# Wo's sixteen low parts: from POOL's queue to DVE's, behind the seventh head's high part

## The chip, the core and the metric

The kernel runs on one core of a Trainium2 chip. The metric is the device time of one execution in microseconds (us), as the median of several runs. The engines are called PE (TensorE matmul), PEld (its weight load), DVE (VectorE), ACT (ScalarE), POOL (GpSimd) and SP (SyncE, which issues the DMAs).

## What is computed

A decoder layer on 16 sequences of 112 tokens, width 1024, with a layer norm behind each of its three parts: a gated feed-forward part that keeps only the larger half of its gate, cross attention to 375 context rows with 32 query heads and 8 key/value heads, and a dequantized 4-bit linear layer. The change lies in the attention:

```
def _L0_xattn_ref(query, key, value, Wq, Wk, Wv, Wo):
    ...
    scores = jnp.einsum('bhqd,bhkd->bhqk', q, k) * scale
    probs = jax.nn.softmax(scores, axis=-1)
    out = jnp.einsum('bhqk,bhkd->bhqd', probs, v)
    out = out.transpose(0, 2, 1, 3).reshape(b, sq, DIM)
    return out @ Wo
```

Products in fp32 are made of three passes in a faster format: an operand is split into a high part, which is its value rounded to that format, and a low part, the fp32 value minus the high part. So each operand needs two element-wise instructions before PE can use it, a cast and a subtraction.

## The kernel before

Four passes run one after the other: the context pass (keys and values), the gated and query pass, `attend_pass` (1839 to 2223 us of the profile) and `finish_pass`. The change is in `attend_pass`.

`attend_pass` goes over 16 batches n (a batch is one sequence) and in each over 8 key/value heads h, each with its 4 query heads. g = 8n + h counts the heads through, x = 3h + t the steps of a batch (24 of them, KT = 3 to a head). At a step PE makes one block of scores (`ap_p_t`, L1663), one third of the product with the values of the head three behind (`ap_p_o`, L1682, or L1676 for a head that isn't split), and at 16 of the 24 steps a pair of matmuls `ap_p_s` (L1648) from which the softmax maximum of the next batch is taken. What each engine does for them:

- ACT: the exponential `ap_e` of each block (L1529), the high part `ap_e_hi` of heads 1, 2 and 4 (L1536), the copy of finished output, and Wo's high parts `wo_wo_hi` (L1547).
- DVE: the maxima of the pairs (L1577, 16 to a batch, called y0 to y15), the high part of heads 0, 5, 6 and 7 (L1591), in batches 4, 8 and 12 a reciprocal (L1597), and the low parts from head 119 on (L1609).
- POOL: the low part `ap_e_lo` of every split head up to 118 (L1509), seven to a batch, since head 3 isn't split.
- Wo comes as 16 half blocks of 128x512 (`ap_wo_raw`, two buffers): two in batch 0 and one in each of batches 1 to 14. ACT makes the high part behind the last exponential of head 6, and POOL the low part (`wo_wo_lo`, L1496), ahead of head 6's own low part. Both are first read in `finish_pass`.

Each engine works through its own queue in the order of the code; nothing reorders it, and semaphores alone hold an instruction back. Pair y of the next batch may be written when the maximum of pair y-2 is taken, because `ap_p_s` has two buffers. Pairs y0 and y1 stand at steps 22 and 23 of a batch, y2 to y15 at steps 1, 2, 4 to 7 and 9 to 16 of the next. `ap_e_hi` and `ap_e_lo` have three buffers, `ap_e` four. PE reads the low part of head g in the middle step of the head g+3.

In the functions printed below, `split_w` of the POOL program makes Wo's low parts, `maxima` and `split_hi` of the DVE program are the instructions that the new one joins, and `first_pair`, `scores` and `values` are PE's.

Of the kernel before, what the change touches and what calls it, by code (L numbers as in the profile page):

```python
# [6 lines left out]
F32 = mybir.dt.float32  # L7
# [4 lines left out]
ALU = mybir.AluOpType  # L12
# [15 lines left out]
H, KV, HD = 32, 8, 32  # L28
REP = H // KV
KT = 3  # L30
# [137 lines left out]
def tile_loads(i):  # L168

    return 2 * (((i + 1) * P - 1) // S - i * P // S + 1) + REP  # L170
# [1154 lines left out]
def attend_pass(nc, cy, kd, vd, qd, w_o, wo_hi, wo_lo, ident_f, od, rd):  # L1325
# [18 lines left out]
    W_LOAD_AT, W_SPLIT_AT = 3, 6  # L1344
# [10 lines left out]
    def hi_by_dve(g):  # L1355
        return split(g) and not hi_by_act(g)

    def lo_by_dve(g):
        return split(g) and g >= KV * (B - 1) - 1

    def lo_by_pool(g):
        return split(g) and not lo_by_dve(g)

    def upto(kind, g):

        return sum(kind(x) for x in range(g + 1))

    def cols(k):
        return slice(D // 2 * (k % 2), D // 2 * (k % 2 + 1))

    def w_parts(n):

        return (0, 1) if n == 0 else (n + 1,) if n < B - 1 else ()

    with ExitStack() as ctx:
# [7 lines left out]
        wo_raw = [m.sb(f"wo_raw{i}", [P, D // 2], F32) for i in range(2)]  # L1383
# [18 lines left out]
        def pairs_at(n, x):  # L1402

            if x in PAIR_OF:
                found = n + 1, PAIR_OF[x]
            elif x - NX in PAIR_OF:
                found = n + 2, PAIR_OF[x - NX]
            else:
                return ()
            return (found,) if found[0] < B else ()  # L1410

        def await_hi(eng, g):
            if not split(g):
                eng.wait_ge(exped, KT * (g + 1))
            elif hi_by_act(g):
                eng.wait_ge(hi_act, upto(hi_by_act, g))
            else:
                eng.wait_ge(hi_dve, upto(hi_by_dve, g))
# [70 lines left out]
        @block.gpsimd  # L1489
        def _(pool):  # L1490
            nc.gpsimd.memset(ks[1][STACK:KR].bitcast(F32), 1.0).then_inc(ones, 1)
            pool.wait_ge(ones, 2)

            def split_w(k):
                pool.wait_ge(wo_hi_done, k + 1)
                nc.gpsimd.tensor_tensor(wo_lo[:, k // 2, cols(k)], wo_raw[k % 2][:], wo_hi[:, k // 2, cols(k)].bitcast(F32),  # L1496
                                        ALU.subtract).then_inc(wo_lo_done, 1)
                pool.wait_ge(wo_lo_done, k + 1)

            for g in range(KV * B):  # L1500
                if g % KV == W_SPLIT_AT:
                    pool.wait_ge(lo_pool, upto(lo_by_pool, g - 1))
                    for k in w_parts(g // KV):
                        split_w(k)
                if lo_by_pool(g):
                    await_hi(pool, g)
                    if g >= NLO:
                        pool.wait_ge(pv, g - NLO + 1)
                    nc.gpsimd.tensor_tensor(e_lo[g % NLO][:], e[g % NE][:], e_hi[g % NHI][:].bitcast(F32),  # L1509
                                            ALU.subtract).then_inc(lo_pool, 1)  # L1510
            pool.wait_ge(cy.hi_done, 1)
            nc.gpsimd.tensor_tensor(cy.o_lo[:], cy.num[:], cy.o_hi[:].bitcast(F32), ALU.subtract).then_inc(cy.lo_done, 1)
# [57 lines left out]
        @block.vector  # L1570
        def _(dve):
            def maxima(n, y):
                h, a = divmod(y, 2)
                if y == 0 and n > 0:
                    dve.wait_ge(nm_turned, n)
                dve.wait_ge(scored, NPAIR * n + y + 1)
                nc.vector.reduce_max(n_max[:, h // 2, 2 * a:2 * a + 2, h % 2], p_s[y % 2][:, :, 0:C], AX_X).then_inc(maxed, 1)  # L1577

            def max_lo(n):
                dve.wait_ge(nmh, n + 1)  # L1580
                nc.vector.scalar_tensor_tensor(out=nm_lo[:], in0=p_s[0][0:H, 0, 384:384 + S], scalar=-1.0,
                                               in1=nm_hi[:].bitcast(F32), op0=ALU.mult,
                                               op1=ALU.subtract).then_inc(nml, 1)

            def split_hi(g):
                dve.wait_ge(exped, KT * (g + 1))
                if g >= NHI:
                    dve.wait_ge(pv, g - NHI + 1)
                if upto(hi_by_dve, g) > 1:
                    dve.wait_ge(hi_dve, upto(hi_by_dve, g) - 1)  # L1590
                nc.vector.tensor_scalar(e_hi[g % NHI][:], e[g % NE][:], 1.0, None, ALU.mult, ALU.add,  # L1591
                                        accum_out=e_sum[:]).then_inc(hi_dve, 1)

            def invert(c):
                for i in range(NO):
                    dve.wait_ge(o_put[i], PUT * cy.pairs_out(i, GB * (c + 1)))
                nc.vector.reciprocal(den[c % 2][:], den[c % 2][:]).then_inc(recip, 1)  # L1597

            def quotients():

                dve.wait_ge(cy.o_loaded[0], 16 * tile_loads(0))
                nc.vector.tensor_tensor(cy.num[:], cy.num[:], cy.add[:], ALU.add)
                dve.drain()
                nc.vector.tensor_tensor(cy.num[:], cy.num[:], cy.rec[:], ALU.mult).then_inc(cy.normed, 1)

            def split_lo(g):
                await_hi(dve, g)
                dve.wait_ge(pv, g - NLO + 1)
                nc.vector.tensor_tensor(e_lo[g % NLO][:], e[g % NE][:], e_hi[g % NHI][:].bitcast(F32),  # L1609
                                        ALU.subtract).then_inc(lo_dve, 1)  # L1610

            def follow(g):
                if hi_by_dve(g):
                    split_hi(g)
                if lo_by_dve(g):
                    split_lo(g)

            for x in range(NX + PAIR_AT[0], NX):
                for pair in pairs_at(-1, x):
                    maxima(*pair)  # L1620
            for n in range(B):
                for x in range(NX):
                    h, t = divmod(x, KT)
                    for pair in pairs_at(n, x):
                        maxima(*pair)
                    if t == 0 and KV * n + h >= 1:
                        follow(KV * n + h - 1)
                    if x == RECIP_AT and n % GB == 0 and n > 0:
                        invert(n // GB - 1)
                    if x == TURN_AT + 2 and n + 1 < B:  # L1630
                        max_lo(n + 1)
                    if n == B - 1 and x == QUOTIENTS_AT:
                        quotients()
            follow(KV * B - 1)

        @block.tensor
# [380 lines left out]
```

## Time and profile before

| what | us |
|---|---|
| median of 3 runs | 2459.7 (2456.05 to 2464.17) |
| the profiled execution, its own time | 2460.78 |
| span of that execution | 2459.0 |
| POOL busy in the span | 1382.4 |
| DVE busy in the span | 1270.6 |

All times of instructions are us from the start of the span. A start and a length of an instruction are as the profiler recorded them; the next instruction of an engine may begin some hundredths before the recorded end of the one ahead. "[0.78 <-ACT ap_e_hi L1536]" behind a row means that the engine was idle for 0.78 us in front of it and that ACT's instruction released it.

### The profile page before, as it was taken

How to read it: one execution, taken by the hardware profiler on the slowest of the kernel's cores; microseconds unless marked ns; L12 is line 12 of the kernel's file. 1: busy time of each engine (PE TensorE's matmuls, PEld its weight loads, DVE VectorE, ACT ScalarE, POOL GpSimd, SP SyncE). 2: the span in 40 equal slices, each digit the busy share in tenths (PEclk: the TensorE clock that was granted, in tenths of full speed). 3: DMA queues.
4: the chain of work that ended last, by engine and by line, in shares of the span. 5: the costliest groups of instructions: out<-in, count | busy, mean ns of one | idle time of the engine just before them, and what ended most of it. 6: DMA issues, size and time to landing. Idle time of an engine off the chain costs nothing. (4 is left out here: it accounts for less than half of the span.)

```text
span 2459.0 us, 33124 instructions
## 1 busy us (share of the span) xinstructions
PE 2403.3 (98%) x12798; PEld 2093.2 (85%) x12798; DVE 1270.6 (52%) x1785; ACT 1045.2 (43%) x1539; POOL 1382.4 (56%) x627
## 2 busy tenths in 40 slices
PE   9999999999999999999999999999999999998998
PEld 9999999988899888999889998899986666666775
DVE  5862304862016940048610269335538888884665
ACT  2112235533337342355333373323327888882111
POOL 5434244866446855448654468445438999971221
PEclk9999999999999999999999999999999999999999
DMA  7656632234323333323343223369986667667672
GB/s 228 193 167 189 197 108 95 104 124 131 111 102 103 127 100 125 109 102 103 116 131 118 94 103 112 107 212 279 297 218 178 189 195 201 181 172 189 174 175 88
DMA packets 256014, 371.74 MB, mean 151 GB/s; under 512 B 127184, under 2 KB 179408, under 8 KB 255600
## 3 DMA queue, kind: packets, MB, share of 16 engines
q1 hardware_dynamic: 255856, 369.61, 49.6%
q8 instruction: 102, 1.67, 0.3%
q14 instruction: 56, 0.46, 0.1%
HBM read 290.15 MB, written 78.70 MB: 150 GB/s over the span
## 5 line engine op out<-in xcount | busy, mean ns | idle before, releaser
L1028 POOL TENSOR_TENSOR gp_w_lo<-cy_raw,gp_w_hi 128x1024 fp32r<-128x1024 f32 (+2 forms) x299 | 721.0, 2412 | 608.5 <-ACT gp_w_hi L903 608.0
L187 PE MATMUL gp_acc<-gp_x_hi,gp_w_hi 128*128 128x448 f32 x1504 | 558.7, 371 | 2.6 <-ACT gp_row L954 2.5
L188 PE MATMUL gp_acc<-gp_x_lo,gp_w_hi 128*128 128x448 f32 x1504 | 550.3, 366 | 0.0
L189 PE MATMUL gp_acc<-gp_x_hi,gp_w_lo 128*128 128x448 f32 x1504 | 550.1, 366 | 0.0
L903 ACT CAST gp_w_hi<-cy_raw 128x1024 fp32r<-128x1024 f32 (+2 forms) x300 | 307.2, 1026 | 314.2 <-PE gp_acc L189 308.4
L1509 POOL TENSOR_TENSOR ap_e_lo<-ap_e,ap_e_hi 125x1344 fp32r<-125x1344 f32 x104 | 317.2, 3082 | 21.3 <-ACT ap_e_hi L1536 14.2
L187 PEld LDWEIGHTS gp_acc<-gp_x_hi,gp_w_hi 128*128 128x128 f32 x1504 | 283.2, 188 | 26.0 <-ACT gp_row L954 4.0
L189 PEld LDWEIGHTS gp_acc<-gp_x_hi,gp_w_lo 128*128 128x128 f32 x1504 | 282.9, 188 | 22.2
L188 PEld LDWEIGHTS gp_acc<-gp_x_lo,gp_w_hi 128*128 128x128 f32 x1504 | 283.3, 188 | 20.9
L514 DVE TENSOR_REDUCE gp_sel_unit<-gp_keys 112x4 f32<-112x2048 f32 x4 | 9.1, 2286 | 547.8 <-ACT gp_keys L915 547.8
L187 PE MATMUL gp_acc<-gp_h_hi,gp_w_hi 128*128 128x448 f32 (+1 forms) x704 | 266.8, 379 | 8.4 <-DVE gp_h_lo L1091 5.6
L189 PE MATMUL gp_acc<-gp_h_hi,gp_w_lo 128*128 128x448 f32 (+1 forms) x704 | 258.3, 367 | 0.0
L188 PE MATMUL gp_acc<-gp_h_lo,gp_w_hi 128*128 128x448 f32 (+1 forms) x704 | 258.0, 366 | 0.0
L1577 DVE TENSOR_REDUCE cy_n_max<-ap_p_s 112x2 f32<-112x750 f32 x240 | 220.2, 936 | 28.8 <-PE ap_p_s L1648 26.3
L1529 ACT ACTIVATE ap_e<-ap_p_t 125x448 f32<-125x448 f32 x384 | 205.5, 546 | 68.7 <-PE ap_p_t L1663 63.6
L507 DVE TENSOR_SCALAR_CACHE_REDUCE gp_keep<-gp_keys,gp_sel_bound 112x2752 bf16<-112x2752 f32 (+1 forms) x56 | 158.2, 2867 | 64.3 <-ACT gp_keys L915 61.7
L341 POOL TENSOR_TENSOR cp_c_lo<-cp_c_raw,cp_c_hi 128x1504 fp32r<-128x1504 f32 x30 | 103.9, 3484 | 140.1 <-ACT cp_c_hi L311 140.1
L921 ACT ACTIVATE gp_act<-gp_acc 128x448 f32<-128x448 f32 x84 | 45.7, 544 | 272.3 <-PE gp_acc L189 272.3
L1663 PE MATMUL ap_p_t<-cy_qs,cy_ks 98*125 98x448 f32 x384 | 156.6, 409 | 0.4 <-DMA cy_qs<-cy_nm_lo 0.3
L187 PEld LDWEIGHTS gp_acc<-gp_h_hi,gp_w_hi 128*128 128x128 f32 (+1 forms) x704 | 132.7, 188 | 23.5 <-DVE gp_h_lo L1091 6.8
L189 PEld LDWEIGHTS gp_acc<-gp_h_hi,gp_w_lo 128*128 128x128 f32 (+1 forms) x704 | 132.5, 188 | 11.7
L188 PEld LDWEIGHTS gp_acc<-gp_h_lo,gp_w_hi 128*128 128x128 f32 (+1 forms) x704 | 132.9, 189 | 10.0
(212 smaller groups left out, 4307.0 us busy)
## 6 DMA issues: line engine op xcount, KB each, us to landing
cy_raw<-in_w_gu SPq DMA_DIRECT2D x172, 512.0 KB, 3.2
cy_raw<-in_w_d SPq DMA_DIRECT2D x80, 512.0 KB, 3.5
cp_c_raw<-in_ctx_t SPq DMA_DIRECT2D x30, 750.0 KB, 7.0
cy_raw<-in_w_q SPq DMA_DIRECT2D x32, 512.0 KB, 4.2
q_scratch<-gp_q_out SPq DMA_DIRECT2D x64, 224.0 KB, 6.3
cy_qs<-q_scratch SPq DMA_DIRECT2D x64, 224.0 KB, 3.4
k_scratch<-cp_k_out SPq DMA_DIRECT2D x32, 376.0 KB
cy_ks<-k_scratch SPq DMA_DIRECT2D x64, 188.0 KB, 3.5
```

The source lines that it names most:

```text
L187: nc.tensor.matmul(out, wh, xh, start=first, stop=False)
L188: nc.tensor.matmul(out, wh, xl, start=False, stop=False)
L189: return nc.tensor.matmul(out, wl, xh, start=False, stop=last)
L341: nc.gpsimd.tensor_tensor(c_lo[p][:, ks(h), :], c_raw[p][:, ks(h), :], c_hi[p][:, ks(h), :].bitcast(F32), ALU.subtract).then_inc(lo_done, 1)
L507: self.nc.vector.tensor_scalar(self.keep[:, b, 0:width], self.keys[:, b, 0:width], bound[:, b:b + 1], None, op, ALU.add, accum_out=self.co ...
L903: last = nc.scalar.copy(o, i)
L921: nc.scalar.activation(act_t[:, c, :], a[:, 0:T], ACT.Silu).then_inc(evac, 1)
L1028: last = nc.gpsimd.tensor_tensor(o, i, hi.bitcast(F32), ALU.subtract)
L1509: nc.gpsimd.tensor_tensor(e_lo[g % NLO][:], e[g % NE][:], e_hi[g % NHI][:].bitcast(F32), ALU.subtract).then_inc(lo_pool, 1)
L1529: nc.scalar.activation(e[g % NE][:, x % KT, :], p_t[x % 2][0:KN, 0:T], ACT.Exp, scale=SCALE).then_inc(exped, 1)
L1577: nc.vector.reduce_max(n_max[:, h // 2, 2 * a:2 * a + 2, h % 2], p_s[y % 2][:, :, 0:C], AX_X).then_inc(maxed, 1)
L1663: nc.tensor.matmul(p_t[x % 2][0:KN, 0:T], ks[p][0:KR, h // 2, h % 2, t * KN:(t + 1) * KN], qs[p][:, h // 2, :, h % 2, :], start=True, stop ...
```

## The change

The subtraction for Wo's half blocks is issued on DVE in place of POOL, with the same operands. It stands at step 21, where the seventh head's (h = 6) high part has just been issued, and waits for ACT's high part of the block. POOL's queue keeps only the low parts of the heads, and loses two waits for itself around each block.

```
@@ POOL's program
-            def split_w(k):
-                pool.wait_ge(wo_hi_done, k + 1)
-                nc.gpsimd.tensor_tensor(wo_lo[:, k // 2, cols(k)], wo_raw[k % 2][:], wo_hi[:, k // 2, cols(k)].bitcast(F32),
-                                        ALU.subtract).then_inc(wo_lo_done, 1)
-                pool.wait_ge(wo_lo_done, k + 1)
-
             for g in range(KV * B):
-                if g % KV == W_SPLIT_AT:
-                    pool.wait_ge(lo_pool, upto(lo_by_pool, g - 1))
-                    for k in w_parts(g // KV):
-                        split_w(k)
@@ DVE's program
+            def split_w(k):
+                dve.wait_ge(wo_hi_done, k + 1)
+                nc.vector.tensor_tensor(wo_lo[:, k // 2, cols(k)], wo_raw[k % 2][:], wo_hi[:, k // 2, cols(k)].bitcast(F32),
+                                        ALU.subtract).then_inc(wo_lo_done, 1)
+
...
+                    if x == KT * (W_SPLIT_AT + 1):
+                        for k in w_parts(n):
+                            split_w(k)
```

POOL's queue in batch 0 before, from head 5's low part on, with what each instruction waits for:

```order
L1509 TENSOR_TENSOR ap_e_lo_18197<-ap_e_18203,ap_e_hi_18194 125x1344 [waits ap_pv,ap_hi_dve]
L1496 TENSOR_TENSOR wo_wo_lo<-ap_wo_raw_18200,wo_wo_hi 128x512 [waits ap_wo_hi_done,ap_lo_pool]
L1496 TENSOR_TENSOR wo_wo_lo<-ap_wo_raw_18201,wo_wo_hi 128x512 [waits ap_wo_hi_done,ap_wo_lo_done]
L1509 TENSOR_TENSOR ap_e_lo_18195<-ap_e_18204,ap_e_hi_18192 125x1344 [waits ap_pv,ap_hi_dve,ap_wo_lo_done]
L1509 TENSOR_TENSOR ap_e_lo_18196<-ap_e_18205,ap_e_hi_18193 125x1344 [waits ap_pv,ap_hi_dve]
```

The same place after; the low parts of heads 5, 6 and 7 now follow one another:

```order
L1499 TENSOR_TENSOR ap_e_lo_18197<-ap_e_18203,ap_e_hi_18194 125x1344 [waits ap_pv,ap_hi_dve]
L1499 TENSOR_TENSOR ap_e_lo_18195<-ap_e_18204,ap_e_hi_18192 125x1344 [waits ap_pv,ap_hi_dve]
L1499 TENSOR_TENSOR ap_e_lo_18196<-ap_e_18205,ap_e_hi_18193 125x1344 [waits ap_pv,ap_hi_dve]
```

DVE's queue in batch 0 before, from the low part of the negated maxima (`cy_nm_lo`) on; 112x2 rows are the maxima, 125x1344 the high parts of heads 6, 7 and 0 of the next batch:

```order
L1581 SCALAR_TENSOR_TENSOR cy_nm_lo<-ap_p_s,cy_nm_hi 32x112 [waits cy_nmh]
L1591 TENSOR_SCALAR ap_e_hi_18192,ap_e_sum<-ap_e_18204 125x1344 [waits ap_hi_dve,ap_pv,ap_exped]
L1577 TENSOR_REDUCE cy_n_max<-ap_p_s 112x2 [waits cy_scored,cy_nm_turned]
L1577 TENSOR_REDUCE cy_n_max<-ap_p_s 112x2 [waits cy_scored]
L1591 TENSOR_SCALAR ap_e_hi_18193,ap_e_sum<-ap_e_18205 125x1344 [waits ap_hi_dve,ap_pv,ap_exped]
L1577 TENSOR_REDUCE cy_n_max<-ap_p_s 112x2 [waits cy_scored] x2
L1591 TENSOR_SCALAR ap_e_hi_18194,ap_e_sum<-ap_e_18202 125x1344 [waits ap_hi_dve,ap_pv,ap_exped]
```

And after; the lines are numbered anew:

```order
L1571 SCALAR_TENSOR_TENSOR cy_nm_lo<-ap_p_s,cy_nm_hi 32x112 [waits cy_nmh]
L1581 TENSOR_SCALAR ap_e_hi_18192,ap_e_sum<-ap_e_18204 125x1344 [waits ap_hi_dve,ap_pv,ap_exped]
L1604 TENSOR_TENSOR wo_wo_lo<-ap_wo_raw_18200,wo_wo_hi 128x512 [waits ap_wo_hi_done]
L1604 TENSOR_TENSOR wo_wo_lo<-ap_wo_raw_18201,wo_wo_hi 128x512 [waits ap_wo_hi_done]
L1567 TENSOR_REDUCE cy_n_max<-ap_p_s 112x2 [waits cy_scored,cy_nm_turned]
L1567 TENSOR_REDUCE cy_n_max<-ap_p_s 112x2 [waits cy_scored]
L1581 TENSOR_SCALAR ap_e_hi_18193,ap_e_sum<-ap_e_18205 125x1344 [waits ap_hi_dve,ap_pv,ap_exped]
```

The two subtractions stand between head 6's high part and the maximum y0, so y0, y1 and head 7's high part are queued behind them. In batches 1 to 14 it is one.

## Rows read from the trace of the kernel before

**Rows 1.** The page: busy time, share of the span, instructions.
```profile
PE 2403.3 (98%) x12798; PEld 2093.2 (85%) x12798; DVE 1270.6 (52%) x1785; ACT 1045.2 (43%) x1539; POOL 1382.4 (56%) x627
```

**Rows 2.** Line L1509: durations in ns (min/median/max); who waited, us and times.
```profile
L1509 POOL TENSOR_TENSOR ap_e_lo<-ap_e,ap_e_hi x104: 3048/3082/3117, 1847.7 to 2199.2; 125x1344 fp32r<-125x1344 f32 x104
...
  PEld ap_p_o L1682: 38.2, 64
  PE ap_p_o L1682: 13.4, 15
```

**Rows 3.** Timeline of POOL (start us, us, engine, line, operation).
```profile
1865.75 2.67 POOL L1496 TENSOR_TENSOR wo_wo_lo<-ap_wo_raw,wo_wo_hi 128x512 fp32r<-128x512 f32 x2
...
1890.71 1.28 POOL L1496 TENSOR_TENSOR wo_wo_lo<-ap_wo_raw,wo_wo_hi 128x512 fp32r<-128x512 f32 x1
...
2008.67 1.29 POOL L1496 TENSOR_TENSOR wo_wo_lo<-ap_wo_raw,wo_wo_hi 128x512 fp32r<-128x512 f32 x1
...
2026.09 6.12 POOL L1509 TENSOR_TENSOR ap_e_lo<-ap_e,ap_e_hi 125x1344 fp32r<-125x1344 f32 x2 [0.78 <-ACT ap_e_hi L1536]
...
2150.34 1.29 POOL L1496 TENSOR_TENSOR wo_wo_lo<-ap_wo_raw,wo_wo_hi 128x512 fp32r<-128x512 f32 x1
...
2168.05 6.09 POOL L1509 TENSOR_TENSOR ap_e_lo<-ap_e,ap_e_hi 125x1344 fp32r<-125x1344 f32 x2 [1.09 <-ACT ap_e_hi L1536]
2174.22 1.28 POOL L1496 TENSOR_TENSOR wo_wo_lo<-ap_wo_raw,wo_wo_hi 128x512 fp32r<-128x512 f32 x1
...
2197.81 1.29 POOL L1496 TENSOR_TENSOR wo_wo_lo<-ap_wo_raw,wo_wo_hi 128x512 fp32r<-128x512 f32 x1
2199.18 3.06 POOL L1509 TENSOR_TENSOR ap_e_lo<-ap_e,ap_e_hi 125x1344 fp32r<-125x1344 f32 x1
```

**Rows 4.** Timeline of DVE in batch 6, from head 6's high part on.
```profile
2006.43 1.55 DVE L1591 TENSOR_SCALAR_CACHE_REDUCE ap_e_hi<-ap_e 125x1344 fp32r<-125x1344 f32 x1 [0.39 <-PE ap_p_o L1676]
...
2007.98 1.83 DVE L1577 TENSOR_REDUCE cy_n_max<-ap_p_s 112x2 f32<-112x750 f32 x2
2009.73 1.54 DVE L1591 TENSOR_SCALAR_CACHE_REDUCE ap_e_hi<-ap_e 125x1344 fp32r<-125x1344 f32 x1
...
2014.37 3.60 DVE L1577 TENSOR_REDUCE cy_n_max<-ap_p_s 112x2 f32<-112x750 f32 x4
```

**Rows 5.** Timeline of ACT in the same batch: Wo's high part.
```profile
2006.07 0.60 ACT L1547 CAST wo_wo_hi<-ap_wo_raw 128x512 fp32r<-128x512 f32 x1
```

**Rows 6.** Timeline of PEld: the weight load of pair y6 in that batch.
```profile
2015.35 0.27 PEld L1648 LDWEIGHTS ap_p_s<-cy_ks,cy_qs 96*112 96x112 f32 x2 [0.28 <-DVE cy_n_max L1577]
```

**Rows 7.** Timelines of DVE (y0) and PEld (y6) in batch 4, with a reciprocal.
```profile
1960.77 0.94 DVE L1577 TENSOR_REDUCE cy_n_max<-ap_p_s 112x2 f32<-112x750 f32 x1
```
```profile
1968.79 0.27 PEld L1648 LDWEIGHTS ap_p_s<-cy_ks,cy_qs 96*112 96x112 f32 x2 [0.94 <-DVE cy_n_max L1577]
```

**Rows 8.** Timelines of DVE (y0) and PE (y6) in batch 12, with a reciprocal.
```profile
2150.01 0.94 DVE L1577 TENSOR_REDUCE cy_n_max<-ap_p_s 112x2 f32<-112x750 f32 x1 [0.35 <-issue]
```
```profile
2158.03 0.61 PE L1648 MATMUL ap_p_s<-cy_ks,cy_qs 96*112 96x376 f32 x2 [0.85 <-DVE cy_n_max L1577]
```

**Rows 9.** Timelines of POOL and DVE in the gated pass.
```profile
515.10 1.17 POOL L1039 TENSOR_TENSOR gp_act<-gp_act,gp_row 128x448 f32<-128x448 f32 x1
518.05 2.40 POOL L1028 TENSOR_TENSOR gp_w_lo<-cy_raw,gp_w_hi 128x1024 fp32r<-128x1024 f32 x1 [1.78 <-ACT gp_w_hi L903]
520.41 1.53 POOL L1039 TENSOR_TENSOR gp_act<-gp_act,gp_row 128x448 f32<-128x448 f32 x1
```
```profile
518.10 2.84 DVE L1091 TENSOR_TENSOR gp_h_lo<-gp_h,gp_h_hi 128x448 fp32r<-128x448 f32 x1
```

**Rows 10.** Line L1091: durations in ns (min/median/max).
```profile
L1091 DVE TENSOR_TENSOR gp_h_lo<-gp_h,gp_h_hi x88: 606/642/2845, 516.8 to 1583.5; 128x448 fp32r<-128x448 f32 x84, 64x448 fp32r<-64x448 f32 x4
```

**Rows 11.** Timeline of DVE: its own low parts of heads 119 and 120.
```profile
2199.35 4.31 DVE L1609 TENSOR_TENSOR ap_e_lo<-ap_e,ap_e_hi 125x1344 fp32r<-125x1344 f32 x1
...
2205.16 1.56 DVE L1609 TENSOR_TENSOR ap_e_lo<-ap_e,ap_e_hi 125x1344 fp32r<-125x1344 f32 x1
```

## The prediction

> **What bounds the kernel now.** I read the page's busy times first, then the line of the low parts, then the timelines of the engines in one batch of the attention pass. The page doesn't decide anything here: POOL has 56% and DVE 52% of the span [rows 1], but these are averages over four passes. In the attention pass POOL sets the pace. Its low parts take 3.08 us each, and PE waited 38.2 us at its weight loads and 13.4 us at its matmuls for them [rows 2]. Its work comes round once a batch: Wo's low part starts at 1890.71 in batch 1 and at 2197.81 in batch 14, thirteen rounds of 23.62 us on the mean [rows 3]. A round of POOL is seven low parts, Wo's subtraction of 1.29 with its 0.08 wait for itself (2008.67 to the next low part), and 0.78 in which it waits for head 4's high part from ACT [rows 3].
>
> The reader should see a second loop beside it, nearly as long, that doesn't go through POOL's arithmetic but through DVE and PE. From y0 on DVE works without a break: y0 and y1 from 2007.98, head 7's high part at 2009.73, four more maxima from 2014.37 [rows 4], and PE waits for one of these (y4) before it may load pair y6, at 2015.35 [rows 6]. From y6 PE goes on to the scores of head 4, ACT makes its exponential and high part, and POOL's low part of head 4 waits for that. Of this loop I take the parts from rows:
>
> - y0's start to y6's start: 2007.98 to 2015.35, 7.37 us [rows 4, 6]. With a reciprocal in between (batches 4, 8 and 12) it is 8.02: 1960.77 to 1968.79 and, again, 2150.01 to 2158.03 [rows 7, 8].
> - y6 to the start of head 4's low part: 2158.03 to 2168.05, 10.02 us [rows 3, 8]. I take it from batch 12 because PE met no wait for POOL in it, so it is PE's own pace.
> - the low parts of heads 4 and 5: 6.10 us (6.09 recorded for the two; Wo's part starts 6.17 behind their start, less some 0.07 of waiting for itself) [rows 3].
>
> Call L the moment at which POOL is free after head 5's low part, 0.07 ahead of the row of Wo's low part. In batch 6 L is 2008.60, and y0 starts at L - 0.62. The second loop is then -0.62 + 7.37 + 10.02 + 6.10 = 22.87, that is 0.75 shorter than POOL's 23.62. It is hidden. Batch 12 shows it bare: there y0 starts at L - 0.26, the sum is -0.26 + 8.02 + 10.02 + 6.10 = 23.88, and the round measured 2150.34 to 2174.22, 23.88 [rows 3, 8].
>
> **What the change removes.** 16 instructions on POOL of 1.29 us with 0.08 of waiting, 1.37 each and 21.9 us in all [rows 3]. If nothing else moved, all of it would come off POOL's path.
>
> **What it adds on DVE.** No row shows this shape on DVE. The nearest is the same subtraction with 448 columns, at 0.606 when undisturbed [rows 10]. With 1344 columns it takes 1.56 [rows 11]. By the slope between the two, 0.95 us for 896 columns, 512 columns take about 0.67 recorded, and the next instruction can start some 0.08 sooner: 0.60. That is not what it will cost, however. At 518.10 this subtraction was started on DVE while POOL was in one of its own, and took 2.84; it ended at 520.94, 0.53 behind the start of POOL's next instruction, which had been queued and whose start was recorded at 520.41 [rows 9]. In the attention pass the same: 4.31 instead of 1.56, when POOL was busy from 2199.18 for 3.06 [rows 3, 11]. So DVE waits until POOL's instruction is over and then gets through first, and the queued POOL instruction pays: 1.53 against 1.17 for the same shape, 0.36 to 0.38 for 448 columns, some 0.45 for 512. The Trainium skill says this in "SBUF — State Buffer", section "Who interferes with whom": a DVE instruction with two SBUF inputs contends with a GpSimd instruction that reads SBUF, and one of them fully blocks. By that rule the trace agrees (2.84 us against 0.61). The maxima and the high parts of rows 4 keep their durations beside POOL.
>
> **Where it lands.** Head 6's high part ends on DVE at 2007.98, Wo's high part has been there since 2006.67 [rows 4, 5], so the subtraction is ready at L - 0.62, in the middle of POOL's low part of head 5, and must wait for L. It ends near L + 0.58, and y0 starts 0.08 sooner, at L + 0.50 (448 columns: 520.94 - 0.08 - 520.41 = 0.45, and 0.05 to 0.07 for 64 more). This holds in every batch: head 6's high part follows PE, and POOL's low parts of heads 4 and 5 start when PE and ACT let them, so their distance stays. Queued behind the subtraction are y0, y1, head 7's high part, y2 and y3, head 0's high part and y4. PE waits for y4. y0 moves from L - 0.62 to L + 0.50, 1.12 later, and only 0.75 of that was slack.
>
> The new round is 0.50 + 7.37 + 10.02 + 6.10 = 23.99, against 23.62: +0.37. POOL's own round would be 23.62 - 1.37 + 0.45 = 22.70, so POOL is no longer what ends last. With a reciprocal: 0.50 + 8.02 + 10.02 + 6.10 = 24.64, against 23.62 twice and 23.88 once: +1.02, +1.02 and +0.76.
>
> **Batch 0** has two subtractions in a row. Before, its round took 1865.75 to 1890.71, 24.96 [rows 3]. After the first one POOL's low part of head 6 is queued and waiting. If it goes first, DVE's second waits for it: y0 at L + 0.45 + 3.05 + 0.50 = L + 4.00, a round of 27.49, +2.53. If DVE runs both at a stretch, y0 is at L + 1.10, a round of 24.59, -0.37. No row shows that case. In rows 9 it was the engine that had waited that came next, so I take +2.53.
>
> **The end.** Behind batch 14's subtraction (L near 2197.74) there are no pairs left. DVE's low part of head 119 waits for POOL's low part of head 118, which starts 1.37 sooner and is held up 0.45: -0.9.
>
> **Sum:** 2.53 + 10 x 0.37 + 1.02 + 1.02 + 0.76 - 0.9 = +8.1 us. The finishing pass keeps its order. The profiled execution took 2460.78 around a span of 2459.0, and would take 2468.9; its time is 1.1 above the median of the three runs, so the median becomes 2459.7 + 8.1 = 2467.8 us. About 0.3%, 7.4 us, is what a measurement of this kernel can tell from no change, so this is on the edge.
>
> **Rivals.**
>
> 1. Batch 0's two subtractions run at a stretch: 2.9 less, +5.2, 2464.9 us. Against it only rows 9, for it that DVE's next instruction is recorded as starting 0.08 before the end of the one ahead.
> 2. POOL stays the bound and the change is a gain. This needs a looser second loop than I read: DVE's delay would have to be taken up before y6, though rows 4 show no gap there. The round is then 22.70, -0.92 in thirteen rounds and some -1.8 in batch 0, with -0.9 at the end: -14.7, 2445.0 us. It decides from a second loop of 22.7 or less, so my loop would be 1.3 too long. Batch 12, where the sum met the measured round, speaks against it. The Trainium skill's "GPSIMD Engine Reference", section "Engine selection", advises it: element-wise work on a tile belongs on VectorE, GpSimd being about twice as slow with two inputs. Rows 10 and 3 agree on the speed (0.67 against 1.29); what they don't give is the port and the place.
> 3. DVE is not blocked at this place. y0 starts at L - 0.02, the round is 23.47, 24.12 with a reciprocal: 10 x -0.15, +0.5, +0.5, +0.24, -0.9 in batch 0, -1.4 at the end, -2.6 us, 2457.1. Against it stand rows 9 and 11.
> 4. DVE loses the turn to POOL's queued low part of head 6 in each batch: y0 at L + 3.55, 3.05 more in thirteen rounds, +48 us, near 2508. Rows 9 show the other order.
>
> **How the numbers follow.** The forecast has 0.45, rival 1 0.27, rival 2 0.12, rival 3 0.10, rival 4 0.06. The round's terms carry 0.1 us or so together, 1.3 us over thirteen rounds, and the first term alone may be 0.45 or 0.60, so the forecast's own range is 2465 to 2471. About a third of it lies below the 0.3% line, and nearly all of rivals 1 and 3: same 0.44. Slower is the rest of the forecast, and rival 4, with a little of rival 1: 0.43. Faster is rival 2 and a little of rival 3: 0.13. The range from 2456 to 2472 holds the forecast, rivals 1 and 3, and leaves out rivals 2 and 4 with 0.18.
>
> **What would show it.** On DVE the sixteen subtractions take between 1.1 and 1.5 us recorded (0.62 of waiting and 0.67), not 0.67, and in batch 0 the second takes some 3.6. POOL's low part of head 6 is recorded at 3.5 instead of 3.08. POOL's idle time in a round grows from 0.8 to 2.1 or so, 1.6 of it in front of head 4's low part. PE no longer waits for POOL's low parts, or for a few us in all in place of 51, and waits for DVE's maxima at y2, y4 and y6 instead. The round of POOL is 24.0, 24.6 at batches 4, 8 and 12. Wrong would be: a round under 23.6; PE still waiting for POOL; subtractions of 0.67 on DVE; or subtractions of more than 3 us in every batch.

## The result, and the profile after

The changed kernel took 2467.8 us in the median of six runs (2463.85 to 2469.41), the kernel before 2459.1 in the seven beside them. The ratio is 1.0035, 95% interval 1.0025 to 1.0045: slower by some 8.6 us, where +8.1 was forecast. One more execution of the changed kernel, slow by far at 12134.81 us, is left out; with it the median is 2468.9, the number that an expectation below quotes. The profiled execution took 2466.65 around a span of 2464.9. The attention pass is 7.9 us longer in it: from POOL's first low part to the finishing pass it was 1847.74 to 2225.92 before, 378.2, and is 1845.08 to 2231.18, 386.1. The finishing pass took 233.7 against 233.1, and the passes ahead of attention happened to end 2.7 earlier.

The page of the changed kernel, busy time, share and instructions of each engine, to be held against [rows 1]:

```profile
PE 2401.3 (97%) x12798; PEld 2095.8 (85%) x12798; DVE 1287.2 (52%) x1801; ACT 1046.1 (42%) x1539; POOL 1369.6 (56%) x611
```

Sixteen instructions moved from POOL to DVE. POOL lost 12.8 us and not the 20.6 of sixteen times 1.29, and DVE gained 16.6 and not the 10.7 of sixteen times 0.67. The other two views show where the rest sits: first the line of POOL's low parts (durations in ns, minimum, median, maximum; what ended POOL's idle time; who waited), then the line of DVE's subtractions.

```profile
L1499 POOL TENSOR_TENSOR ap_e_lo<-ap_e,ap_e_hi x104: 3050/3086/3552, 1845.1 to 2203.9; 125x1344 fp32r<-125x1344 f32 x104
...
  ACT ap_e_hi L1526: 26.8, 16
  DVE ap_e_hi L1581: 15.6, 15
...
  PEld ap_p_o L1680: 0.8, 1
  PE ap_p_o L1680: 0.4, 1
```
```profile
L1604 DVE TENSOR_TENSOR wo_wo_lo<-ap_wo_raw,wo_wo_hi x16: 1222/1229/3520, 1862.1 to 2203.3; 128x512 fp32r<-128x512 f32 x16
```

PE's waits for POOL's low parts have gone: 0.8 us and 0.4 in place of the 38.2 and 13.4 of [rows 2]. The waits of the attention pass (1842 to 2210; us in all, times, longest) name who took POOL's place:

```profile
PEld ap_p_s L1646 <- DVE cy_n_max L1567: 30.9, 32, 3.8
POOL ap_e_lo L1499 <- ACT ap_e_hi L1526: 26.8, 16, 2.6
PE ap_p_s L1646 <- DVE cy_n_max L1567: 24.5, 31, 3.4
```

Batch 6 shows one round. DVE's timeline from the subtraction on, PEld's at pair y6, and POOL's over the round (start us, us; in brackets the idle time ahead and what ended it), beside [rows 3, 4, 6]:

```profile
2010.77 1.22 DVE L1604 TENSOR_TENSOR wo_wo_lo<-ap_wo_raw,wo_wo_hi 128x512 fp32r<-128x512 f32 x1
2011.92 1.77 DVE L1567 TENSOR_REDUCE cy_n_max<-ap_p_s 112x2 f32<-112x750 f32 x2
...
2034.63 1.24 DVE L1604 TENSOR_TENSOR wo_wo_lo<-ap_wo_raw,wo_wo_hi 128x512 fp32r<-128x512 f32 x1
```
```profile
2019.22 0.27 PEld L1646 LDWEIGHTS ap_p_s<-cy_ks,cy_qs 96*112 96x112 f32 x2 [1.37 <-DVE cy_n_max L1567]
```
```profile
2005.36 9.58 POOL L1499 TENSOR_TENSOR ap_e_lo<-ap_e,ap_e_hi 125x1344 fp32r<-125x1344 f32 x3 [1.68 <-ACT ap_e_hi L1526]
2015.24 12.37 POOL L1499 TENSOR_TENSOR ap_e_lo<-ap_e,ap_e_hi 125x1344 fp32r<-125x1344 f32 x4 [0.29 <-DVE ap_e_hi L1581]
2029.22 9.60 POOL L1499 TENSOR_TENSOR ap_e_lo<-ap_e,ap_e_hi 125x1344 fp32r<-125x1344 f32 x3 [1.61 <-ACT ap_e_hi L1526]
```

The subtraction starts at 2010.77, in the middle of POOL's low part of head 5, and ends at 2011.99, some 0.5 behind that part's end (2005.36 and twice 3.05 give 2011.46). It had been started by then, so it was no semaphore that held it back. POOL's three low parts then last 9.58 instead of 9.16 or so: 3.48 for the third. POOL waits 1.61 ahead of head 4 in place of 0.78. The round is 2010.77 to 2034.63, 23.86.

Batch 0 has two subtractions. DVE's, PE's and POOL's timelines there, then two windows (length, busy time and instructions of PE, PEld, DVE, ACT and POOL, the granted clock, DMA share, GB/s):

```profile
1862.08 4.67 DVE L1604 TENSOR_TENSOR wo_wo_lo<-ap_wo_raw,wo_wo_hi 128x512 fp32r<-128x512 f32 x2
```
```profile
1867.66 0.97 PE L1646 MATMUL ap_p_s<-cy_ks,cy_qs 96*112 96x376 f32 x2 [3.35 <-DVE cy_n_max L1567]
1868.42 0.57 PE L1661 MATMUL ap_p_t<-cy_qs,cy_ks 98*125 98x448 f32 x1
...
1874.27 0.36 PE L1661 MATMUL ap_p_t<-cy_qs,cy_ks 98*125 98x448 f32 x1
```
```profile
1869.99 6.24 POOL L1499 TENSOR_TENSOR ap_e_lo<-ap_e,ap_e_hi 125x1344 fp32r<-125x1344 f32 x2 [3.79 <-DVE ap_e_hi L1581]
```
```profile
1863.00:1868.00 5.00, 1.65 (x8) 1.00 (x7) 5.00 (x4) 1.57 (x4) 3.21 (x1) 0.88 0.93 273
1868.00:1875.00 7.00, 7.00 (x24) 5.49 (x24) 6.55 (x9) 2.92 (x6) 4.89 (x2) 0.60 0.57 145
```

The two subtractions took 4.67 together, PE stood for 3.35 behind them, and the clock fell from 2.4 to 1.2 GHz, at the end of that wait already (0.88 over 1863 to 1868): matmuls of 448 columns last 0.57 instead of 0.36, until some 1873.7. Before, PE stood 2.08 at most behind 1863 and kept a clock of 1.00.

A mark that every kernel below has is DVE's row on cy_nm_lo, once a batch. The round of batch 0 from these is 1862.86 to 1887.82 before, 24.96, and here:

```profile
1859.95 0.26 DVE L1571 SCALAR_TENSOR_TENSOR cy_nm_lo<-ap_p_s,cy_nm_hi 32x112 fp32r<-32x112 f32 x1 [0.47 <-ACT cy_nm_hi L1509]
1888.48 0.26 DVE L1571 SCALAR_TENSOR_TENSOR cy_nm_lo<-ap_p_s,cy_nm_hi 32x112 fp32r<-32x112 f32 x1 [0.47 <-ACT cy_nm_hi L1509]
...
1960.16 0.26 DVE L1571 SCALAR_TENSOR_TENSOR cy_nm_lo<-ap_p_s,cy_nm_hi 32x112 fp32r<-32x112 f32 x1 [0.47 <-ACT cy_nm_hi L1509]
1984.76 0.26 DVE L1571 SCALAR_TENSOR_TENSOR cy_nm_lo<-ap_p_s,cy_nm_hi 32x112 fp32r<-32x112 f32 x1 [0.47 <-ACT cy_nm_hi L1509]
```

Batch 0's takes 28.53, batch 4's, with a reciprocal, 24.60.

### The profile page after: what moved, and what is told of

Same layout as the page of the kernel before. It is cut to its first block and busy times, and to the rows that moved or that the text cites. A ratio compares the mean times of both kernels' runs of the same rounds, so it can differ in the third digit from the quotient of the medians.

```text
span 2464.9 us, 33107 instructions
## 1 busy us (share of the span) xinstructions
PE 2401.3 (97%) x12798; PEld 2095.8 (85%) x12798; DVE 1287.2 (52%) x1801; ACT 1046.1 (42%) x1539; POOL 1369.6 (56%) x611
## 5 line engine op out<-in xcount | busy, mean ns | idle before, releaser
L1499 POOL TENSOR_TENSOR ap_e_lo<-ap_e,ap_e_hi 125x1344 fp32r<-125x1344 f32 x104 | 324.6, 3148 | 43.7 <-ACT ap_e_hi L1526 26.8
L187 PEld LDWEIGHTS gp_acc<-gp_h_hi,gp_w_hi 128*128 128x128 f32 (+1 forms) x704 | 132.7, 188 | 23.2 <-DVE gp_h_lo L1091 6.8
L1646 PE MATMUL ap_p_s<-cy_ks,cy_qs 96*112 96x376 f32 x480 | 127.2, 347 | 25.0 <-DVE cy_n_max L1567 24.8
```

The lines of the kernel that those rows point to most:

```text
L187: nc.tensor.matmul(out, wh, xh, start=first, stop=False)
L1646: last = nc.tensor.matmul(p_s[y % 2][:, i, 0:CP], qs[p][0:STACK, f, 2 * a + i, h % 2, :], ks[p][0:STACK, f, h % 2, :], start=True, stop=True)
```

## The experiments

Theory: a subtraction on DVE waits for the end of the low part that POOL is in, and gets through ahead of POOL's next (called **the port** here). It so delays the maxima for which PE waits, and a **second loop** through DVE, PE and ACT, 22.87 us long when nothing delays it, sets the round. The rivals: the delay is only DVE's added work; POOL's arithmetic is still the bound; batch 0 is slow for another reason.

| run | median, before, us | ratio (95%) | plain round | round with reciprocal |
|---|---|---|---|---|
| changed kernel | 2467.8, 2459.1 | 1.0035 (1.0025 to 1.0045) | 23.9 | 24.6 |
| e1_one_input | 2457.75, 2458.09 | 0.9998 (0.9989 to 1.0008) | 23.35 | 24.05 |
| e2_two_quarters | 2511.32, 2458.09 | one run | 26.9 (28.0 in two) | 27.5 |
| e3_batch0_pool | 2462.32, 2458.09 | 1.0019 (1.001 to 1.0029) | 23.9 | 24.6 |
| e9_batch0_shared | 2465.75, 2460.4 | 1.0023 (1.0013 to 1.0032) | 23.9 | 24.6 |
| e7_act_copy | 2451.26, 2458.09 | 0.9977 (0.9968 to 0.9987) | 22.95 | 23.5 |
| e4_pool_ahead_of_4 | 2452.09, 2458.58 | 0.9977 (0.9968 to 0.9986) | 22.9 | 23.5 |
| e5_dve_before_y14 | 2453.24, 2458.58 | 0.9977 (0.9964 to 0.9989) | 22.9 | 23.5 |
| e6_pool4_recip20 | 2449.99, 2458.58 | 0.9967 (0.9955 to 0.9979) | 22.9 | 23.0 |
| e8_dve14_recip20 | 2453.76, 2460.4 | 0.997 (0.9959 to 0.9982) | 22.9 | 23.0 |

The rounds are those of most batches. e4, e5, e6 and e8 each have one or two that are 0.2 to 0.4 longer, at different batches. Batch 12's took 23.9 in the kernel before, in e7 and in e4, where DVE stood 0.35 for "issue" in front of y0 [rows 8], and 23.5 in e5. Why is open.

### One SBUF input instead of two (e1_one_input)

```diff
-                nc.vector.tensor_tensor(wo_lo[:, k // 2, cols(k)], wo_raw[k % 2][:], wo_hi[:, k // 2, cols(k)].bitcast(F32),
-                                        ALU.subtract).then_inc(wo_lo_done, 1)
+                if k > 0:
+                    dve.wait_ge(wo_lo_done, k)
+                nc.vector.tensor_scalar(wo_lo[:, k // 2, cols(k)], wo_raw[k % 2][:], 1.0, None, ALU.mult, ALU.add,
+                                        accum_out=w_sum[:]).then_inc(wo_lo_done, 1)
```

> From the changed kernel: DVE's instruction for Wo's half block stands at the same place and writes the same block, but reads one tensor in SBUF (a multiply by 1 with a sum, the form of the high parts) in place of two, so the low part isn't computed. Theory P (the port): the instruction takes 0.67 us recorded in place of 1.23, since it needn't wait for POOL; y0 starts 0.55 sooner behind head 6's high part, the round is 13.94 + 1.48 + 0.60 + 7.30 = 23.3 us (23.86 in the changed kernel), and batch 0's two take 1.3 together in place of 4.67. In all 10 x 0.55 + 3 x 0.55 + 3.5 = 10 to 11 us less than the changed kernel, 2458 us, about the time of before. Rival W (it is DVE's added work and its place, the port has no part in it): the round stays at 23.8 and the time at 2466 to 2469.

DVE's line of the sixteen instructions:

```profile
L1607 DVE TENSOR_SCALAR_CACHE_REDUCE wo_wo_lo<-ap_wo_raw x16: 679/681/686, 1864.1 to 2193.9; 128x512 fp32r<-128x512 f32 x16
```

The place, the queue and the size are the same; the second input from SBUF is gone, and with it the instruction has another form. The form isn't what counts: e5 below has the two-input subtraction at 0.68 as well, where POOL idles. The instruction takes 0.68, not 1.22 and never 3.52, also in batch 0; POOL's low parts are 9.16 for three. The round is 23.35 and the time that of the kernel before, to 0.1%. So DVE's added work alone doesn't make the kernel slower than before. It does lengthen the second loop, from 22.93 (e7, below) to 23.35, which is still under the 23.6 of before; the wait for POOL adds the other 0.54 and brings the round to 23.89. That this form passes POOL and the one with two inputs does not is as the Trainium skill's "SBUF — State Buffer", section "Who interferes with whom", has it.

### Two instructions of half the width (e2_two_quarters)

```diff
+                for i in range(2 if k >= 2 else 1):
+                    q = D // 4 if k >= 2 else D // 2
+                    c = D // 2 * (k % 2) + q * i
+                    done = nc.vector.tensor_tensor(wo_lo[:, k // 2, c:c + q], wo_raw[k % 2][:, q * i:q * i + q],
+                                                   wo_hi[:, k // 2, c:c + q].bitcast(F32), ALU.subtract)
+                done.then_inc(wo_lo_done, 1)
```

> From the changed kernel: in batches 1 to 14 the subtraction is two instructions of 256 columns, one behind the other, in place of one of 512. The work is the same but for some 0.1 us. Theory P, with the turn going to the engine that has waited: the first ends near L + 0.3, POOL's low part of head 6 goes next, and the second waits 3.05 us for it; y0 starts some 3.0 later than in the changed kernel, each round is 26.8 to 26.9, and the whole 40 to 44 us longer, near 2510 us. Rival S (DVE keeps the port for instructions at a stretch; batch 0's long second subtraction had another cause): the round stays within 0.2 of 23.9 and the time near 2470.

DVE's subtractions in batch 6, PE's matmuls of the scores behind the wait in batches 5 to 7, and the windows of the rounds of batches 0, 5, 6 and 7, each from mark to mark:

```profile
2027.44 4.15 DVE L1607 TENSOR_TENSOR wo_wo_lo<-ap_wo_raw,wo_wo_hi 128x256 fp32r<-128x256 f32 x2
```
```profile
2005.68 0.59 PE L1650 MATMUL ap_p_s<-cy_ks,cy_qs 96*112 96x376 f32 x2 [2.91 <-DVE cy_n_max L1567]
2032.50 0.97 PE L1650 MATMUL ap_p_s<-cy_ks,cy_qs 96*112 96x376 f32 x2 [2.80 <-DVE cy_n_max L1567]
2060.50 0.60 PE L1650 MATMUL ap_p_s<-cy_ks,cy_qs 96*112 96x376 f32 x2 [2.91 <-DVE cy_n_max L1567]
```
```profile
1862.90:1890.30 27.40, 23.98 (x106) 17.04 (x105) 25.25 (x27) 19.73 (x39) 21.82 (x8) 0.94 0.63 166
1998.48:2025.31 26.83, 22.52 (x106) 16.08 (x105) 24.75 (x28) 19.74 (x38) 21.54 (x8) 1.00 0.63 170
2025.31:2053.29 27.98, 25.18 (x106) 18.03 (x105) 25.06 (x27) 19.48 (x38) 21.58 (x8) 0.88 0.62 163
2053.29:2080.23 26.94, 23.98 (x106) 16.97 (x105) 24.76 (x28) 19.43 (x38) 21.53 (x8) 0.94 0.62 170
```

The same number of elements in two pieces costs 2.96 us a round (26.82 against 23.86): behind the first piece POOL's queued low part goes first, and the second piece waits for all of it. So between two instructions of DVE the engine that waits gets the turn. This was the open point in batch 0, and it is answered against rival 1.

The windows show more. PE's waits in batches 1 to 12 all lie between 2.80 and 2.93, but the granted clock of the round is 1.00 in two of them, 0.94 in eight and 0.88 in two. A short fall costs at most 0.1 (26.94 against 26.83), the long one 1.1 (27.98). In the long one the first matmul behind the wait is slow already (0.97); in the short ones it is at full speed, and the slow matmuls begin 1 to 3 us later.

Batch 0 is the same code here as in the changed kernel, with the same 4.67 of DVE and the same wait of 3.35. It took 27.40 with a clock of 0.94, where the changed kernel's took 28.53 with 0.88. What differs in the rows is how long the clock was low, so 1.13 of the 28.53 belong to that execution's clock.

### Batch 0's two back on POOL (e3_batch0_pool), or one of them (e9_batch0_shared)

```diff
-                    if x == KT * (W_SPLIT_AT + 1):
+                    if n > 0 and x == KT * (W_SPLIT_AT + 1):
```

and POOL's two subtractions of batch 0 as they were. The second run:

```diff
+                if g == W_SPLIT_AT:
+                    pool.wait_ge(lo_pool, upto(lo_by_pool, g - 1))
+                    pool.wait_ge(wo_lo_done, 1)
+                    split_w(1)
...
-                        for k in w_parts(n):
+                        for k in (0,) if n == 0 else w_parts(n):
```

> From the changed kernel: batch 0's two subtractions are POOL's again, the other fourteen stay on DVE. Theory P: batch 0's round goes from 28.5 us back to 25.0, the others stay at 23.86 (24.6 with a reciprocal): 3.5 us less than the changed kernel, some 4 us above before, 2463 to 2464 us. PE has no wait of over 3 us, and the granted clock in the 28 us behind batch 0's step 21 is 1.0 in place of 0.88. Rival: the later rounds make up for what batch 0 loses (slack behind it), then the time stays within 1 us of the changed kernel's.

> The changed kernel, but in batch 0 alone POOL makes the second of the two low parts, behind DVE's first and ahead of head 6's low part. What is told apart: whether batch 0 costs what it does (its round 28.5 us in place of 25.0, the 3.5 us instead of the forecast 2.53) because a second subtraction on DVE waits for a whole low part of POOL and PE, waiting 3.35 us behind it, loses its clock. By that: DVE's one subtraction there takes 1.2 us, PE waits for a maximum for less than 1.5 us in batch 0, no granted clock under 1.00 behind it, the round of batch 0 is 24 to 25 us, and the time 3.5 to 4.5 us under the changed kernel's 2468.9 less what the days differ: 2463 to 2464.5 beside 2459 for the kernel before. By the rival, that the clock falls there whatever DVE does (it is a slow stretch at the start of the pass), the clock's dip stays, the round is 25 to 26, and the time 2465 to 2466.

In the second run, DVE in batch 0 and the marks of its round, then the window behind:

```profile
1863.06 0.26 DVE L1581 SCALAR_TENSOR_TENSOR cy_nm_lo<-ap_p_s,cy_nm_hi 32x112 fp32r<-32x112 f32 x1 [0.47 <-ACT cy_nm_hi L1519]
...
1865.19 1.24 DVE L1614 TENSOR_TENSOR wo_wo_lo<-ap_wo_raw,wo_wo_hi 128x512 fp32r<-128x512 f32 x1
...
1887.25 0.26 DVE L1581 SCALAR_TENSOR_TENSOR cy_nm_lo<-ap_p_s,cy_nm_hi 32x112 fp32r<-32x112 f32 x1 [0.47 <-ACT cy_nm_hi L1519]
```
```profile
1868.00:1875.00 7.00, 5.57 (x28) 4.06 (x27) 7.00 (x10) 4.60 (x9) 7.00 (x3) 1.00 1.02 272
```

With one subtraction on DVE, batch 0's round is 24.19, its clock stays at 1.00 and PE waits 1.16 at most; with none it is 24.97. The rival, a stretch that is slow by itself, has fallen. The other rounds are 23.9 in both, so what is left in e3's ratio, 4.7 us, is the change's steady part. The step from 1.0035 to 1.0019 is 3.9 us, and the traces say 3.56 (28.53 against 24.97). The second run's median, 2465.75, lies in the range that its rival named, and not in the one expected; the kernel before took 2460.4 beside it, and by the ratio it is 5.7 us slower than before, where 4 to 5.5 were expected. It is the trace that decides against the rival. That trace is 4.34 shorter in batch 0 than the changed kernel's, the ratio only 0.0012 lower, 3 us, and no lower than e3's; the intervals leave room for both.

### No port, no POOL: a copy on ACT (e7_act_copy)

```diff
                 nc.scalar.copy(wo_hi[:, k // 2, cols(k)], wo_raw[k % 2][:]).then_inc(wo_hi_done, 1)
+                nc.scalar.copy(wo_lo[:, k // 2, cols(k)], wo_raw[k % 2][:]).then_inc(wo_lo_done, 1)
```

and DVE's subtractions left out.

> Neither POOL nor DVE makes Wo's low parts: ACT makes a second copy of the raw block in their place, behind the high part (0.52 us on ACT each, the low part isn't computed). It shows what taking the work off POOL is worth with DVE left alone. Theory L (the loop over DVE's maxima and PE is next, 22.8 to 22.9 us, 23.5 with a reciprocal): the round is 22.8 to 23.2, PE still waits little for POOL, and the time is 2459.1 - (0.4 to 0.8) x 13 - 2 = 2447 to 2452 us. Rival F (POOL alone sets the pace and all of its 1.37 us comes back): the round is 22.25, the time 2459.1 - 21 = 2438 us.

POOL's timeline over two rounds:

```profile
1995.87 21.35 POOL L1499 TENSOR_TENSOR ap_e_lo<-ap_e,ap_e_hi 125x1344 fp32r<-125x1344 f32 x7 [1.65 <-ACT ap_e_hi L1526]
2018.79 21.32 POOL L1499 TENSOR_TENSOR ap_e_lo<-ap_e,ap_e_hi 125x1344 fp32r<-125x1344 f32 x7 [1.57 <-ACT ap_e_hi L1526]
2041.73 6.10 POOL L1499 TENSOR_TENSOR ap_e_lo<-ap_e,ap_e_hi 125x1344 fp32r<-125x1344 f32 x2 [1.63 <-ACT ap_e_hi L1526]
```

POOL has only its seven low parts, 21.35, and nothing of Wo stands on DVE either. Still the round is 22.92 to 22.94, and POOL idles for 1.6 of it ahead of head 4. This is the second loop bare: 22.87 was worked out from rows of the kernel before, 22.93 is what it takes. So the change could not have gained more than some 0.7 a round, wherever its subtractions went, as long as the reciprocal stays where it is.

### Other places for the same subtraction (e4, e5, e6, e8)

POOL's own, but ahead of head 4's low part, where POOL idles (e4_pool_ahead_of_4, from the kernel before):

```diff
-                if g % KV == W_SPLIT_AT:
+                n, h = divmod(g, KV)
+                parts = w_parts(0) if g == W_SPLIT_AT else (n,) if n >= 2 and h == 4 else ()
+                if parts:
```

DVE's, but between the maxima of y13 and y14 of the next batch, when POOL idles (e5_dve_before_y14; batch 0's two on POOL):

```diff
+                    if x == 15 and n >= 2:
+                        split_w(n)
```

And each of the two with the reciprocal moved from between y0 and y6 to behind the low half of the maxima (e6_pool4_recip20, e8_dve14_recip20):

```diff
-                    if x == RECIP_AT and n % GB == 0 and n > 0:
+                    if x == TURN_AT + 2 and n % GB == 0 and n > 0:
```

> From the kernel before: the subtractions stay on POOL, but those of batches 1 to 14 are made in the next batch, ahead of head 4's low part, where POOL stands idle for 0.8 us a round waiting for ACT. Batch 0's two stay where they were. Theory L (POOL's queue and the loop over DVE's maxima and PE, 22.8 us): POOL's own round is 7 x 3.05 + 1.37 = 22.7, the other loop's 13.94 + 1.48 + 7.30 = 22.7 to 22.8, 23.5 with a reciprocal; so the round falls from 23.62 to 22.8, and the time by 10 x 0.8 + 0.6 + 1.4 = 10 us to 2449 us. Rival (the idle time ahead of head 4 is no slack, since the low part of head 4 behind it is what PE needs next): the round stays at 23.6 and the time at 2459.

> DVE makes the subtraction as in the changed kernel, but for batches 2 to 15 at step 15, ahead of the maximum y14, a third of a batch before POOL's busiest stretch; batch 0's two are POOL's as before. Ahead of y14 nothing needs y14 and y15 at once but the transpose at step 18. Theory P: the cost is now the delay of that transpose, 0.4 to 1.3 us, by how long DVE waits for POOL's low part; the round is 23.2 to 23.9, the time 2453 to 2461 us, and the subtraction takes 0.7 to 2.5 us recorded, since POOL is in the middle of a low part there. Rival W (any 0.6 us on DVE costs the same wherever it stands): round 23.86 and 2463.5 us, like the changed kernel without batch 0's part.

> As the kernel with POOL's subtraction ahead of head 4's low part, and in batches 4, 8 and 12 the reciprocal stands at step 20, behind the low part of the negated maxima, where DVE waits 0.4 us for PE, in place of step 22 between y0 and y1. Theory L: these three rounds lose 0.65 in front of y6 and gain 0.35 in front of head 6's high part: 23.2 in place of 23.5, the time 0.9 us less than without it, 2448 us. Rival: the reciprocal was hidden there, no difference.

> The kernel with DVE's subtraction between the maxima of y13 and y14 of the next batch (batch 0's two on POOL), and the reciprocal moved behind the low half of the maxima as in the run with POOL's subtraction ahead of head 4. By the theory of the second loop (22.87 a round; the reciprocal costs 0.65 only where it stands between y0 and y6), the rounds of batches 4, 8 and 12 fall from 23.5 to 22.9, and the time to 2451 to 2452 beside 2459, some 1.9 us under the 2453.2 without that move. If the reciprocal at its new place holds up the high part of head 3 or 4, the rounds stay at 23.5 and the time at 2453.

POOL in e4, then POOL and DVE in e5:

```profile
1992.75 1.29 POOL L1496 TENSOR_TENSOR wo_wo_lo<-ap_wo_raw,wo_wo_hi 128x512 fp32r<-128x512 f32 x1
1994.27 21.34 POOL L1511 TENSOR_TENSOR ap_e_lo<-ap_e,ap_e_hi 125x1344 fp32r<-125x1344 f32 x7 [0.22 <-POOL wo_wo_lo L1496]
2015.68 1.29 POOL L1496 TENSOR_TENSOR wo_wo_lo<-ap_wo_raw,wo_wo_hi 128x512 fp32r<-128x512 f32 x1
```
```profile
2020.95 21.34 POOL L1509 TENSOR_TENSOR ap_e_lo<-ap_e,ap_e_hi 125x1344 fp32r<-125x1344 f32 x7 [1.75 <-ACT ap_e_hi L1536]
2043.83 3.06 POOL L1509 TENSOR_TENSOR ap_e_lo<-ap_e,ap_e_hi 125x1344 fp32r<-125x1344 f32 x1 [1.54 <-ACT ap_e_hi L1536]
```
```profile
2019.78 0.68 DVE L1614 TENSOR_TENSOR wo_wo_lo<-ap_wo_raw,wo_wo_hi 128x512 fp32r<-128x512 f32 x1
...
2042.66 0.68 DVE L1614 TENSOR_TENSOR wo_wo_lo<-ap_wo_raw,wo_wo_hi 128x512 fp32r<-128x512 f32 x1
```

In e4 the subtraction sits in what was POOL's idle time: its round is 22.93 with the same instructions as before (23.62). In e5 DVE's subtraction falls into POOL's idle time, 2019.20 to 2020.95, and takes 0.68, the price by the slope of [rows 10, 11] in all fourteen batches. The maxima behind it are those of y14 and y15, and head 4's exponential and high part don't wait for them: POOL starts head 4 at 2020.95, as ready, and the round is 22.88. So the same instruction on the same engine costs 1 us less a round than in the changed kernel, by its place alone. That isn't what was expected of e5: a wait for POOL (0.7 to 2.5 us recorded) and rounds of 23.2 to 23.9. By the ratios both gain 5.7 us. Of e4 10 were expected, 0.8 a round; by the marks the ten rounds behind batch 0 take 230.59 (1881.99 to 2112.58) in place of 236.00 (1887.82 to 2123.82), 5.4 less or 0.54 a round. The plain ones came down by 0.7, those with a reciprocal by 0.1 alone, and the first by 0.3.

The reciprocal costs where it stood, between y0 and y6, and nothing at its new place: batch 4's round, by the marks of e4 and then of e6,

```profile
1951.07 0.26 DVE L1583 SCALAR_TENSOR_TENSOR cy_nm_lo<-ap_p_s,cy_nm_hi 32x112 fp32r<-32x112 f32 x1 [0.48 <-ACT cy_nm_hi L1521]
1974.59 0.26 DVE L1583 SCALAR_TENSOR_TENSOR cy_nm_lo<-ap_p_s,cy_nm_hi 32x112 fp32r<-32x112 f32 x1 [0.48 <-ACT cy_nm_hi L1521]
```
```profile
1955.07 0.26 DVE L1583 SCALAR_TENSOR_TENSOR cy_nm_lo<-ap_p_s,cy_nm_hi 32x112 fp32r<-32x112 f32 x1 [0.47 <-ACT cy_nm_hi L1521]
1978.04 0.26 DVE L1583 SCALAR_TENSOR_TENSOR cy_nm_lo<-ap_p_s,cy_nm_hi 32x112 fp32r<-32x112 f32 x1 [0.48 <-ACT cy_nm_hi L1521]
```

fell from 23.52 to 22.97, and from 23.51 to 22.97 between e5 and e8: 0.55, by the forecast's term 0.65. The 0.35 that e6 was expected to lose at the new place doesn't show. The ratios of e6 and e8, 0.9967 and 0.997, are the lowest of the study: both beat the kernel before by 7 to 8 us and the changed one by some 16, though by less than expected (2448 and 2451 to 2452 us). Between the two, and between each and its version without the move, the intervals don't decide.

## Why the prediction was right, and where it was off

**The kind of case was right.** The time went the way of the forecast and not of a rival. Rival 2 (POOL stays the bound) asked for rounds of 22.70; e7 shows that even without any subtraction the round is 22.93. Rival 3 (no blocking) would have been the rounds of e1, 23.35, and e1 shows what had to be missing for it: the second input. Rival 4 (the turn is lost in each batch) would have cost what e2 does by its second piece, +53 us. Rival 1 (batch 0 at a stretch) fell by the second subtraction of 3.52 us.

**One argument had no weight.** That batch 12's sum met the measured round was taken as proof of the loop. All its terms and y0's start were read in that one batch, one behind the other, so they add up to the round whatever bounds it. The test is e7: 22.93, where 22.87 had been put together from two batches.

**The plain rounds.** Forecast 23.99, +0.37; measured 23.86 to 23.91 against 23.56 to 23.63 by the marks, +0.30 on the mean. By its terms in batch 6: y0 starts at L + 0.46 (0.50 forecast), y0 to y6 took 2011.92 to 2019.22, 7.30 (7.37), y6 to head 4's low part 2019.22 to 2029.22, 10.00 (10.02), the two low parts 6.10. Their sum is 23.86. The step that was 0.07 too long is y0 to y6: behind the delay DVE had all its inputs at hand (y0 and y1 take 1.77 in place of 1.83). Over ten rounds that is 0.7 us.

**The reciprocal rounds.** Forecast +1.02, +1.02, +0.76; measured +1.01 (24.60 against 23.59), +0.94 (24.57 against 23.63) and +0.70 (24.59 against 23.89).

**Batch 0.** Forecast +2.53, measured +3.57. The turn was called rightly, from [rows 9], and e2 and e9 confirm it. The term was 1.04 too small since it took PE's pace behind the wait from rows at full clock. PE stood for 3.35 us, its clock fell to the lower level, and some 17 matmuls ran at 0.37 from start to start and not 0.20. Both subtractions are in the forecast rightly: y0 starts 6.73 behind the mark in the changed kernel and in e2, and with e2's shorter fall the round is 27.40, where 27.49 was forecast. So how much the term missed by depends on the execution that one looks at. The trace of the kernel before held a warning that the prediction didn't read. At the start of the same pass, PE's timeline and the window behind it:

```profile
1848.49 0.59 PE L1648 MATMUL ap_p_s<-cy_ks,cy_qs 96*112 96x376 f32 x2 [1.47 <-DVE cy_n_max L1577]
...
1851.77 0.57 PE L1682 MATMUL ap_p_o<-ap_e_hi,cy_vs 125*66 125x448 f32 x1
...
1854.45 0.37 PE L1663 MATMUL ap_p_t<-cy_qs,cy_ks 98*125 98x448 f32 x1
```
```profile
1850.00:1863.00 13.00, 13.00 (x55) 9.28 (x54) 10.20 (x13) 9.98 (x19) 10.27 (x5) 0.87 0.41 117
```

The clock falls there too, behind short waits. A forecast that puts a wait of over 3 us in front of PE should have had the clock as a term, from these rows.

**The end.** Forecast -0.9. From the last L to the finishing pass it was 28.2 before (2197.74 to 2225.92) and is 27.2 (2203.99 to 2231.18), -1.0. DVE's low part of head 119, the 4.31 of [rows 11], now takes 2.87:

```profile
2206.03 2.87 DVE L1599 TENSOR_TENSOR ap_e_lo<-ap_e,ap_e_hi 125x1344 fp32r<-125x1344 f32 x1
```

**The sum.** 3.57 + 10 x 0.30 + 1.01 + 0.94 + 0.70 - 1.0 = 8.2, beside 7.9 for the whole pass (the stretch ahead of batch 0's mark is 0.25 shorter). Two terms were off by +1.0 and -0.7 and nearly cancelled; that the forecast came within 1 us of the measurement owes something to this.

**What would show it.** The list held: subtractions of 1.22 to 1.25 and one of 3.52; POOL's low part of head 6 at 3.48 to 3.55; POOL idle for 1.9 a round (2.1 forecast), 1.6 of it ahead of head 4; PE waiting 0.8 us for POOL and 30.9 for the maxima; rounds of 23.9 and 24.6.

**The chances.** That the result would lie just at the 0.3% line was seen; "same" was given a hair more than "slower", and the measurement put it a hair over the line, which its interval (0.25% to 0.45%) has inside.

## What to carry to other kernels

Moving an instruction from the bounding engine to one that is half idle pays only up to the next loop. Add that loop up, term by term, from rows of batches in which its parts show bare, test the sum on a batch whose rows it wasn't read from, and ask what the moved instruction delays at its new place: here the forecast had a slack of 0.75 us and a delay of 1.12, and the delay came out at 1.08.

In these runs the subtraction with two inputs from SBUF was cheap on DVE only where POOL was idle. The same instruction cost 0.68 in POOL's gap, 1.22 across the end of a POOL instruction, and 3.52 right behind another of its kind; splitting it made it dearer. Look first for the bounding engine's own idle time: putting POOL's subtraction there, with no change of engine, gained as much as any other place.

## What the runs showed of the hardware that was not expected

**The turn changes between two DVE instructions, even back to back.** DVE's first ended some 0.5 us behind POOL's low part, and its second had been queued; POOL's next low part still went first, and the second took 3.52 us. In e2 two pieces of 256 columns took 4.15 together, where one of 512 took 1.22.

**The clock's fall doesn't follow from the wait's length alone.** Behind 3.35 us in batch 0 the granted clock was 0.60 over 7 us in the changed kernel, and the round 1.13 longer than in e2, where it fell behind the same wait for a shorter time. In e2, waits of 2.80 to 2.93 were followed by a long fall in two rounds of twelve, by a short one in eight and by none in two. Behind 2.08 in batch 0 of the kernel before it stayed at 1.00. Yet behind 1.47, at the start of the pass, it fell in the kernel before (0.87 over 13 us) and not in e1, which had the same 1.47 there and 1.00 throughout. What decides between such cases was not tried and is left open. What it costs depends on the place: a short fall cost 0.1 in a round of e2, while the stretch ahead of batch 0's mark, mark to mark, took 29.97 in the kernel before and 28.47 in e1.

**The spread between executions goes with the clock.** The changed kernel's two shortest runs (2463.85 and 2464.16) had a mean granted clock of 0.996, its two longest (2468.98 and 2469.41) of 0.994. Whether the clock accounts for all of the difference isn't shown.
